# The opening of a fused layer-norm, cross-attention and feed-forward kernel: four tiles normalised on ScalarE, GpSimd's opening work in another order, one exchange into another scratch tile

## What is computed

```python
x = x + xattn(layernorm(x), ctx, ctx, pos, mask, Wq, Wk, Wv, Wo)
x = x + ffn(layernorm(x), ffn_kernel, ffn_bias)

def xattn(query, key, value, pos, mask, Wq, Wk, Wv, Wo):
    q = (query @ Wq).reshape(nb, q_len, H, D).transpose(0, 2, 1, 3)
    k = (key @ Wk).reshape(nb, q_len, KVH, D).transpose(0, 2, 1, 3)
    v = (value @ Wv).reshape(nb, q_len, KVH, D).transpose(0, 2, 1, 3)
    q = q * cos + rotate_half(q) * sin
    k = k * cos + rotate_half(k) * sin
    scores = einsum('bhqd,bhkd->bhqk', q, repeat(k)) / sqrt(D)
    scores = where(mask == 0, -1e9, scores)
    return (softmax(scores) @ repeat(v)).reshape(nb, q_len, H * D) @ Wo
```

## Time and profile before

| | us |
|---|---|
| median of 3 runs | 1160.65 |
| lowest, highest | 1158.66, 1161.06 |
| the profiled execution's own time | 1159.31 |
| its span | 1157.1 |

### The profile page before, as it was taken

The page is one execution under the profiler, slowest core; times in us unless marked ns, Lnnn a source line. Parts: engine busy times, 40 slices in busy tenths (PEclk is TensorE's granted clock), DMA queues, the critical chain, the costliest instruction groups (busy, mean ns, idle before and its releaser), DMA issues.

```text
span 1157.1 us, 19685 instructions
## 1 busy us (share of the span) xinstructions
PE 1133.6 (98%) x6340; PEld 974.4 (84%) x6340; DVE 818.6 (71%) x1747; ACT 762.5 (66%) x2297; POOL 636.7 (55%) x524
## 2 busy tenths in 40 slices
PE   4999999999999999999999999999999999999998
PEld 3788888888888888888888888888888888888876
DVE  7777777777777777678887766656666665666687
ACT  4576766667776766777766566766766676666663
POOL 6864644455453655569766456454555446544433
PEclk9999999999999999999999999999999999999999
DMA  7211301111010111134112121110201111020001
GB/s 231 80 56 38 92 15 33 60 42 64 25 60 24 45 61 38 46 101 144 53 51 82 64 84 55 28 56 19 82 2 37 47 37 64 12 71 19 2 6 68
DMA packets 51748, 63.47 MB, mean 55 GB/s; under 512 B 8768, under 2 KB 27584, under 8 KB 51648
## 3 DMA queue, kind: packets, MB, share of 16 engines
q1 hardware_dynamic: 50736, 59.86, 17.0%
q0 software_dynamic: 768, 2.10, 0.6%
q10 hardware_dynamic: 144, 0.26, 0.1%
HBM read 58.01 MB, written 4.19 MB: 54 GB/s over the span
## 4 chain that ended last, share of the span: by engine, by line
PE 92%; POOL 3%; DVE 2%; issue 2%; ACT 1%; POOLq 0%; DVEq 0%; ACTq 0%
PE proj L464 14%; PE proj L465 14%; PE proj L466 14%; PE pS L564 9%; PE pO L616 8%; PE pO L617 8%; PE pO L618 8%; PE pV L594 3%; PE pV L595 3%; PE pT L577 2%; PE pO L626 2%; PE proj L509 1%; PE proj L515 1%; PE pO L629 1%; PE proj L478 1%
## 5 line engine op out<-in xcount | busy, mean ns | idle before, releaser
L783 ACT CAST PS<-pT 64x256 fp32r<-64x256 f32 x256 | 93.8, 367 | 299.3 <-PE pV L595 296.1
L1129 POOL TENSOR_TENSOR t<-t,SIN 128x512 f32<-128x512 f32 x128 | 165.2, 1291 | 194.1 <-ACT t L752 193.5
L464 PE MATMUL proj<-XH,QH 128*128 128x512 f32 x512 | 202.2, 395 | 1.6 <-DVE XL L858 1.5
L466 PE MATMUL proj<-XH,QL 128*128 128x512 f32 x512 | 200.1, 391 | 0.0
L465 PE MATMUL proj<-XL,QH 128*128 128x512 f32 x512 | 200.1, 391 | 0.0
L616 PE MATMUL pO<-OH,AH 128*128 128x512 f32 x432 | 171.5, 397 | 0.0
L1134 POOL TENSOR_TENSOR qT<-qT,t 128x512 f32<-128x512 f32 x128 | 165.5, 1293 | 10.1
L617 PE MATMUL pO<-OL,AH 128*128 128x512 f32 x432 | 169.1, 392 | 0.0
L618 PE MATMUL pO<-OH,AL 128*128 128x512 f32 x432 | 168.3, 390 | 0.0
L905 DVE TENSOR_TENSOR qT<-proj,COS 128x512 f32<-128x512 f32 x128 | 88.3, 690 | 96.3 <-PE proj L466 57.7
L792 ACT ACTIVATE pS<-pS,tiny 128x64 f32<-128x64 f32 x512 | 142.9, 279 | 12.9 <-DVE tiny L1049 8.8
(11 more groups left out here) (189 smaller groups left out, 2558.3 us busy)
## 6 DMA issues: line engine op xcount, KB each, us to landing
QR<-wq SPq DMA_DIRECT2D x64, 256.0 KB, 2.7
OR<-wo SPq DMA_DIRECT2D x62, 256.0 KB, 3.0
CR<-ctxT SPq DMA_DIRECT2D x16, 256.0 KB, 4.5
KR<-wk SPq DMA_DIRECT2D x16, 256.0 KB, 2.6
UR<-wv SPq DMA_DIRECT2D x16, 256.0 KB, 3.5
acc<-x SPq DMA_DIRECT2D x15, 256.0 KB, 3.1
out<-acc SPq DMA_DIRECT2D x15, 256.0 KB, 2.0
rawx<-x SPq DMA_DIRECT2D x8, 256.0 KB, 2.8
```

Of the source, the lines that this page charges most:

```text
L464: pe.matmul(dst, lh, rh, start=k == 0, stop=False)
L466: made = pe.matmul(dst, ll, rh, start=False, stop=k == last)
L1129: pool.tensor_tensor(t[:, :], t[:, :], SIN[:, 512 * (s % 2):512 * (s % 2) + 512], ALU.mult).then_inc(g_qs, 1)
```

## The change

- The gather indices take three VectorE operations instead of five.
- `normalise` for x tiles 4 to 7 moves to ScalarE (`x_normalise`: scale and shift in one activation), two at step 0 behind the casts of stream 0, one each at steps 1 and 2. VectorE makes the shift (`shift_mean`), and takes the statistics of tiles 4 to 7 ahead of the loop. GpSimd makes their inverse deviations in pairs.
- In the opening, GpSimd's `gather(3)` goes behind `inverse(3)`, a wait for the fourth normalised tile and two lows; `gather(7)` and the key weights' low go behind the first rotation.
- x tiles 5 to 7 are loaded earlier, the first value weights are listed at step 4.
- Exchange 1 goes into `t3` and waits for no rotation; the first key rotation (which also uses `t3`) waits for rotation 1.
- VectorE's context lows stand behind `times_cos` (steps 0 and 4) and behind the maximum (step 5). GpSimd's first key rotation stands ahead of the lows of step 4.

```diff
     out = [(-1, "q", 0, 0), (-1, "q", 0, 1), (0, "q", 0, 2), (0, "c", 0, 0), (0, "q", 0, 3), (0, "c", 0, 1),
-           (0, "c", 0, 2), (0, "c", 0, 3), (0, "k", 0, 0), (3, "v", 0, 0), (3, "v", 1, 0), (4, "c", 1, 0),
+           (0, "c", 0, 2), (0, "c", 0, 3), (0, "k", 0, 0), (4, "v", 0, 0), (4, "v", 1, 0), (4, "c", 1, 0),
            (4, "c", 1, 1), (5, "c", 1, 2), (5, "c", 1, 3)]
...
         st6, mv0, ve0, rs0 = tiny[:, 0:6], tiny[:, 6:8], tiny[:, 8:9], tiny[:, 9:10]
-        mhalf = tiny[:, 10:11]
+        mhalf = tiny[:, 24:26]
+        shift = tiny[:, 16:20]
         nmx, rsum, rinv = tiny[:, 12:16], tiny[:, 16:20], tiny[:, 20:24]
...
+        a_xn = sem("a_xn")
...
         v_lo, v_xl, v_qc, v_kc, v_ks = sem("v_lo"), sem("v_xl"), sem("v_qc"), sem("v_kc"), sem("v_ks")
+        v_sh = sem("v_sh")
         v_sm, v_mx, v_ri, v_pn, v_pl, v_al = sem("v_sm"), sem("v_mx"), sem("v_ri"), sem("v_pn"), sem("v_pl"), sem("v_al")
...
-            return t3 if i == PAIRS - 1 else t2
+            return t3 if i in (1, PAIRS - 1) else t2
...
-            if T is not None and T < 4:
-                return amax[:, 2 * T:2 * T + 2], amax[:, 8 + T:9 + T], amax[:, 12 + T:13 + T]
+            if T is not None and T < 8:
+                a = amax if T < 4 else pw
+                return a[:, 2 * (T % 4):2 * (T % 4) + 2], a[:, 8 + T % 4:9 + T % 4], a[:, 12 + T % 4:13 + T % 4]
             return mv0, ve0, rs0
-        ln_order = [("x", T) for T in range(4)]
+        ln_order = [("x", T) for T in range(8)]
         for n in range(FIRST, END):
-            if n in X_AT:
+            if n in X_AT and X_AT[n] >= 8:
                 ln_order.append(("x", X_AT[n]))
...
+        def rs_count(kind, i):
+            at = LN[kind, i]
+            return at + 1 if at < 4 else at // 2 + 3 if at < 8 else at - 1
...
         def _(sp):
-            def load_stream(n):
-                for i in streamed(n):
+            def load_stream(some):
+                for i in some:
                     _, kind, a, b = STREAM[i]
...
             load_x(3)
-            load_stream(-1)
+            load_stream(streamed(-1))
             load_x(4)
-            load_stream(0)
-            for T in range(5, 8):
-                load_x(T)
+            load_x(5)
+            load_stream(streamed(0)[:3])
+            load_x(6)
+            load_x(7)
+            load_stream(streamed(0)[3:])
             for n in range(FIRST, END):
                 if n:
-                    load_stream(n)
+                    load_stream(streamed(n))
                 if n + 1 in X_AT and X_AT[n + 1] >= 8:
...
                 b = bank(("x", T))
-                pe.wait_ge(v_xn, T + 1)
+                if 4 <= T < 8:
+                    pe.wait_ge(a_xn, T - 3)
+                else:
+                    pe.wait_ge(v_xn, T + 1 if T < 4 else T - 3)
                 turn(b, x_norm(T), 4).then_inc(e_xt, 1)
...
+            def x_normalise(T):
+                _, _, rs = ln_place(T)
+                act.wait_ge(v_sh, T - 3)
+                act.activation(x_norm(T), x_source(T), ACT.Identity, bias=shift[:, T - 4:T - 3],
+                               scale=rs).then_inc(a_xn, 1)
...
                     act.wait_ge(g_kr, STEPS)
-                elif i:
+                elif i > 2:
                     act.wait_ge(g_qr, i)
+                elif i == 2:
+                    act.wait_ge(g_qr, 1)
                 else:
...
                 if n == 0:
+                    x_normalise(4)
+                    x_normalise(5)
                     for T in range(4):
                         rope(T)
+                if n == 1:
+                    x_normalise(6)
+                if n == 2:
+                    x_normalise(7)
...
             def normalise(kind, i):
-                at = LN[kind, i]
                 mv, _, rs = ln_place(i if kind == "x" else None)
-                dve.wait_ge(g_rs, at + 1)
+                dve.wait_ge(g_rs, rs_count(kind, i))
                 if kind == "x":
...
+            def shift_mean(T):
+                mv, _, rs = ln_place(T)
+                dve.wait_ge(g_rs, rs_count("x", T))
+                dve.tensor_scalar(shift[:, T - 4:T - 3], mv[:, 0:1], rs, -1.0, ALU.mult, ALU.mult).then_inc(v_sh, 1)
...
                 else:
-                    dve.wait_ge(e_ct, 4)
+                    dve.wait_ge(g_qr, 2)
                 dve.tensor_tensor(t3[0:64, :], proj[64:128, b, :], SIN[64:128, c], ALU.mult)
...
             dve.wait_ge(d_pos, 16)
-            dve.tensor_copy(amax, idx.bitcast(I32)).then_inc(v_idx, 1)
+            dve.tensor_scalar(pw, idx.bitcast(I32), 0.0, 512.0, ALU.is_lt, ALU.mult).then_inc(v_idx, 1)
             dve.wait_ge(v_idx, 1)
-            dve.tensor_scalar(pw, amax, 0.0, 512.0, ALU.is_lt, ALU.mult).then_inc(v_idx, 1)
+            dve.tensor_tensor(amax, idx.bitcast(I32), pw, ALU.add).then_inc(v_idx, 1)
             dve.wait_ge(v_idx, 2)
-            dve.tensor_tensor(amax, amax, pw, ALU.add).then_inc(v_idx, 1)
-            dve.wait_ge(v_idx, 3)
-            dve.tensor_scalar(pw, amax, 0.0, 511.0, ALU.max, ALU.min).then_inc(v_idx, 1)
-            dve.wait_ge(v_idx, 4)
-            dve.tensor_copy(idx.bitcast(U32), pw).then_inc(v_idx, 1)
+            dve.tensor_scalar(idx.bitcast(U32), amax, 0.0, 511.0, ALU.max, ALU.min).then_inc(v_idx, 1)
             statistics("x", 0)
...
             normalise("x", 2)
-            x_low(0)
             normalise("x", 3)
-            for T in range(1, 4):
+            for T in range(4):
                 x_low(T)
+            for T in range(4, 8):
+                statistics("x", T)
             for n in range(FIRST, END):
...
                         last_sums()
-                if n in X_AT:
+                if n in X_AT and X_AT[n] >= 8:
                     statistics("x", X_AT[n])
...
                 if n == 0:
+                    for T in range(4, 6):
+                        shift_mean(T)
                     low(lows.pop(0))
-                if n in X_AT and (X_AT[n] < 8 or X_AT[n] % 4 == 3):
+                    for T in range(6, 8):
+                        shift_mean(T)
+                if n in X_AT and X_AT[n] >= 8 and X_AT[n] % 4 == 3:
                     normalise("x", X_AT[n])
-                for i in lows:
-                    low(i)
                 if n == 4:
...
                     times_cos(BANK["q", n], qT[:, s % 2, :, h, :], s % 2).then_inc(v_qc, 1)
+                if n < 5:
+                    for i in lows:
+                        low(i)
                 if 0 <= m < PAIRS:
...
                                       negate=True).then_inc(v_mx, 1)
+                if n == 5:
+                    for i in lows:
+                        low(i)
                 if n in FFN_AT and FFN_AT[n] == 8:
...
                     pool.wait_ge(v_const, 1)
-                pool.tensor_tensor(rs, ve, mhalf, ALU.pow).then_inc(g_rs, 1)
+                pool.tensor_tensor(rs, ve, mhalf[:, 0:1], ALU.pow).then_inc(g_rs, 1)
+            def inverse_pair(T):
+                pool.wait_ge(v_stat, 3 * LN["x", T + 1] + 3)
+                pool.tensor_tensor(pw[:, 8 + T:10 + T], pw[:, 4 + T:6 + T], mhalf, ALU.pow).then_inc(g_rs, 1)
...
                 if T == 0:
-                    pool.wait_ge(v_idx, 5)
+                    pool.wait_ge(v_idx, 3)
                 if T == 8:
...
                 inverse("x", T)
-            gather(3)
             inverse("x", 3)
+            pool.wait_ge(v_xn, 4)
             low(PLACE["q", 0, 0])
             low(PLACE["q", 0, 1])
+            gather(3)
             gather(4)
-            inverse("x", 4)
+            inverse_pair(4)
+            low(PLACE["q", 0, 2])
             gather(5)
-            low(PLACE["q", 0, 2])
+            inverse_pair(6)
             low(PLACE["q", 0, 3])
             gather(6)
-            gather(7)
-            low(PLACE["k", 0, 0])
             for n in range(FIRST, END):
...
                     add_bias(FFN_AT[n])
-                if n in X_AT and n:
+                if n in X_AT and X_AT[n] >= 8:
                     inverse("x", X_AT[n])
...
                     rotate_q(n - 1)
+                if n == 1:
+                    gather(7)
+                    low(PLACE["k", 0, 0])
+                if n == 4:
+                    rotate_k(0)
                 for i in lows:
...
                     gather(ROPE_AT[n] + 2)
-                if k_step(n) is not None:
+                if k_step(n):
                     rotate_k(k_step(n))
```

## The result

| | before | after |
|---|---|---|
| median, us | 1159.70 (4 runs) | 1153.82 (4 runs) |
| lowest, highest | 1158.66, 1161.06 | 1152.96, 1155.82 |
| profiled execution, its span | 1159.31, 1157.1 | 1155.82, 1153.6 |

The ratio is 0.9953 [0.9937, 0.9969], 5.4 us faster (5.9 by the medians, one more run of before among them than at the prediction). Forecast were 4.7 us and 1155.3; the time is in the range and in the forecast's case.

The account below looks back on a forecast made before the run. TensorE, busy in 98% of the span, was taken as the bound, so only its unfilled time before the second scores could be won: 1160.0 - 4.7 = 1155.3 us, range 1152.2 to 1159.6.

Parts of the forecast that it names:

- The landmark and the base: Gain counted at TensorE's second scores (54.21 us before), kept from there on; starting time taken as 1160.0 us.
- Part 1: Opening up to the first projection: it can start at 14.1 us, 3.3 us earlier.
- Part 2: Up to the second projection: ScalarE's normalises wait behind the key weights' cast; start near 22.5 instead of 23.34, 0.8 us won.
- second table load: ScalarE's early normalises: a further activation table load bounded at 0 to 1.28 us, taken as 0.
- Here most of those 3.3 us stop counting: Between first and second projection: of the 3.3 us won at the first, only 0.8 us remain at the second.
- slow pace: TensorE at the 1.2 GHz level after a gap: up to 1.6 us, possible ahead of the second projection or behind first scores.
- Part 3: Second projection to first scores: GpSimd's row counts, key rotation ends at 40.8, first scores at 41.4 to 42.4 instead of 46.66.
- new wait for the value lows: Ahead of the first value projection: TensorE waits 1 us for lows ending at 43.4 without disturbance, included in the sum.
- Part 4: First to second scores: VectorE's context lows enter at GpSimd's next instruction boundary; second scores at 49.5 for 54.21, 4.7 us gained.
- Locked out: VectorE's context lows wait for GpSimd's whole row; softmax ends at 53.6, 0.6 us won, 1159.4 us; chance 22%.
- slower: Lockout also catches lows c12 and c13, TensorE resumes at 1.2 GHz; 3.9 us lost, 1163.9 us; chance 8%.
- nothing in the way: Context lows slip into GpSimd's row at no cost; second scores at 47.6, 6.6 us won, 1153.4 us; chance 15%.

Follow-up runs that it names:

- e_control: The changed kernel run again without any edit, on a second chip; median 1154.03 us, ratio 0.9948 to the kernel before.
- e_undo_pool: Changed kernel with GpSimd's opening in the old order: gather(3) ahead of the fourth inverse, no wait for the fourth normalised tile; 1155.86 us, ratio 0.9966 to the kernel before.
- e_warm8: Changed kernel plus eight 128x512 matmuls with unread results, ahead of TensorE's wait for the value lows; 1152.69 us, ratio 0.9944 to the kernel before.
- e_dve_norm: Changed kernel with x tiles 4 to 7 normalised by VectorE where it made their shifts, not by ScalarE; 1152.90 us, ratio 0.9942 to the kernel before.

## Why the prediction was right

**The landmark and the base.** That the gain is what the second scores win was right: 4.5 us in the traces (forecast 4.7), the rest of the span the same to 0.4 us in every kernel but for the gap at 557.8. The time was 1.5 us below the forecast. Of that 0.3 to 0.9 us are the base, 1160.0, where four runs of before have 1159.7 and the 47 beside the experiments medians of 1158.88 to 1159.22. The rest can be estimated: the execution nearest the median has a span of 1151.6, less 1102.6 behind the second scores, so these stood near 49.0 in it, 0.5 us ahead of the forecast, and what follows them was 0.3 us shorter than in the trace of before. Executions that keep the full clock come lower still (1152.42 and 1152.46 in e_control).

**Part 1** was right and slightly too careful: 13.66 against 14.1.

**Part 2** had the order of events right, and its sizes off by some tenths: the cast of the key weights began at 18.87 and not 19.8, `gather(3)` let the fourth cosine turn go on at 19.37 and not 20.1, and ScalarE's normalise takes 0.8 us, not the 0.6 taken from a cast:

```profile
18.87 0.62 ACT L701 CAST KH<-KR 128x512 fp32r<-128x512 f32 x1 [0.18 <-DMA KR<-wk]
19.40 1.51 ACT L714 ACTIVATE qT<-acc,tiny 128x512 f32<-128x512 f32 x2
```

The second projection was at 21.91 for 22.5. There was no second table load (one in the whole trace, 1283 ns), as the Trainium skill, ScalarE: Activation LUTs, Table sets, has it. What failed in this part is the sentence "Here most of those 3.3 us stop counting": e_undo_pool puts 1.64 us on them, since with the old opening ScalarE's normalises wait for their shifts and not for the weights. That the end of the first projection counts for little, as the forecast had it, is shown by e_control: there it ran at full pace from its start (13.85) and was done by 16.7, where in after it took until 18.1, and the second projection came 0.15 us earlier. The gap ahead of the second projection was in two pieces (0.43 at 19.37, 1.47 at 21.28) and brought no slow pace.

**Part 3** was right to 0.6 us: key rotation 40.73 (40.8), first scores 40.83 (41.4). It gave the exchange in t3 no price; at the first scores it is 1.3 us, by way of exchange 2 and the key projection's bank. The new wait for the value lows was forecast at 1 us and is 1.98, as the scores came 0.6 earlier and the value lows, stretched by c10 and c11, 0.24 later than the 43.4 that was put for them without disturbance.

**Part 4** gave the right number for a partly wrong reason. The lows entered at the next boundary, as forecast, four times out of four. The Trainium skill, SBUF — State Buffer, section Who interferes with whom, has a VectorE instruction with two SBUF inputs and a GpSimd one that reads SBUF exclude each other for a whole instruction. The trace agrees with it in these four rows. "Locked out" and "slower" are refuted here; why the row at 19.88 of the earlier trace rows waited for two GpSimd instructions stays open. But c10 came at 38.50 and got in behind rotation 3, one boundary earlier than in the sum, so the softmax was done at 47.66, 1.3 to 2.4 us before the 48.95 to 50.05 from which the forecast was taken. TensorE's own work, put at 48.6 at full pace, would have had the second scores at 48.1. What carried them to 49.71 was the slow pace, which the prediction had in a sentence about the first scores and as an upper bound, not as the likeliest. The step that failed is thus the new wait ahead of the first value projection's short matmuls: it was costed at its length, 1 us, and not at the clock that it brings, as the earlier trace rows (0.51 from 48 to 51.4) showed for a wait of 1.84 us in the kernel before. Two errors of opposite sign, -1.4 and +1.6, gave 49.71 for 49.5: that the two numbers agree so closely is luck.

**The rival "nothing in the way"** (47.6 us for the second scores) came near for a reason it didn't have: executions at a full clock, e_warm8 with 47.83, are there, although all four lows were lengthened.

## What to carry to other kernels

Find the instruction from which the bound engine never waits again and account every edit to its start: what edits won at earlier landmarks (3.8, 1.4, 5.8 us) was neither the sum nor the order of what they were worth there. Where an edit makes a new wait for the bound engine, look at the granted clock behind it as well as at the wait, and if the wait can't be removed, fill it with work of no use, no longer than the wait. Take one part of a change back at a time: here taking back the order of VectorE's lows cost most, and taking back the move of four normalises to another engine nothing. What a part costs when it is taken back holds beside the other parts, and such costs need not add up to the gain.

## What the runs showed of the hardware

- The changed kernel (e_control) runs with and without a stretch at 1.2 GHz behind a 1.98 us wait and short matmuls, from one execution to the next: 1152.4 us at a mean clock of 1.000, 1154.0 to 1155.8 at 0.997 to 0.999. Eight matmuls in the wait kept the clock in 19 of 19 executions of four kernels, four in 4 of 5 (with an earlier value low besides). Why the clock falls in one execution of the same program and not in the next is not shown.
- The kernel before has two groups of times too, about 1158.7 to 1159.5 and 1160.1 to 1161.1, which its mean clock doesn't tell apart (0.998 in both). What does was not tried.
- A normalise on ScalarE with a scale and a bias for each row, 128x512, takes 0.8 us, a cast of the same shape 0.62.
- One load of 256 KB took 4.8, 5.5 and 5.9 us in three executions at the same place. Behind the slowest TensorE idled 1.29 us, behind the others not at all.
- A VectorE low that came 0.12 us behind the start of a GpSimd instruction waited for it (e_dve_norm), one that came 0.50 us ahead of the same instruction got in before it (after): the softmax behind them ended 1.2 us apart.
